# Vision tower on one core: a step's matrix work reordered around the score blocks, slot results a step later, the second key and query halves as paired 64-row products

## The reference, cut to what matters

```python
h = patches(x) @ W.T                                   # (64, 196, 768) -> (64, 196, 192)
q, k, v = silu(h @ Wq), silu(h @ Wk), silu(h @ Wv)      # 12 heads of 16
out = ((q @ k.T) * decay) @ v                           # decay: causal, exp(slope * distance)
out = layernorm((out * sigmoid(h @ Wg1 @ Wg2)) @ Wo, ln_w, ln_b)
h = layernorm(h + out)
xn = rms_norm(h) * norm_weight
logits = (l2_normalize(slots) * scale) @ l2_normalize(xn).T     # (64 slots, 196 tokens)
y = softmax(logits, over tokens) @ xn                   # 64 slot inputs for each image
y = gelu(y @ fc1[s] + fc1_bias[s]) @ fc2[s] + fc2_bias[s]       # weights of their own for each slot
h = layernorm(h + softmax(logits, over slots).T @ y)
```

## Time and profile before

| | |
|---|---|
| median of 3 runs | 1220.68 us (1220.43 to 1223.71) |
| the profiled execution, its own time | 1220.71 us |
| its span from first to last instruction | 1219.0 us |
| busy, share of the span | PE 91%, DVE 65%, ACT 62%, POOL 49% |
| phase 1 | from the start to about 938 us |
| mean granted TensorE clock | 0.958 of 2.4 GHz |

### The profile page before, as it was taken

How to read it: one execution, slowest core, us unless ns; L and a number is a source line. 1 busy time by engine, 2 the same in 40 slices (tenths; PEclk the granted TensorE clock), 3 DMA queues, 4 the chain that set the end, 5 groups by cost and what they waited for, 6 DMA issues and landing times.

```text
span 1219.0 us, 35974 instructions
## 1 busy us (share of the span) xinstructions
PE 1105.5 (91%) x13418; PEld 889.2 (73%) x13418; DVE 787.8 (65%) x2082; ACT 750.0 (62%) x1745; POOL 595.9 (49%) x942
## 2 busy tenths in 40 slices
PE   4899999999999999999999999999998999997563
PEld 3787888888888888888888888788886556564332
DVE  5577766677777777676777777777774222222996
ACT  5567677777777776777777777776763111110676
POOL 3366655565555666555655555665533000000664
PEclk9999999999999999999999999999999999998555
DMA  4411121111111111211111111112063999995786
GB/s 151 197 51 55 58 84 59 62 53 53 53 53 53 53 53 55 80 66 61 55 53 53 53 53 53 53 53 77 32 263 129 368 424 423 424 423 181 235 264 183
DMA packets 50718, 158.41 MB, mean 130 GB/s; under 512 B 5386, under 2 KB 31392, under 8 KB 38372
## 3 DMA queue, kind: packets, MB, share of 16 engines
q1 hardware_dynamic: 33080, 145.09, 32.2%
q10 hardware_dynamic: 17600, 12.78, 3.4%
HBM read 132.23 MB, written 25.62 MB: 129 GB/s over the span
## 4 chain that ended last, share of the span: by engine, by line
PE 71%; DVE 22%; issue 2%; ACT 1%; DVEq 1%; SPq 1%; DMA 1%; POOL 0%; ACTq 0%; POOLq 0%
DVE p_sb L828 9%; PE ps L974 8%; PE ps L976 7%; PE ps L975 7%; PE ps L1271 6%; PE ps L1052 5%; PE ps L1089 4%; PE ps L1290 4%; PE ps L1134 4%; DVE gn L803 3%; PE ps L1031 3%; PE ps L1032 3%; PE ps L1019 2%; PE ps L1157 2%; DVE res L943 2%
## 5 line engine op out<-in xcount | busy, mean ns | idle before, releaser
L427 POOL TENSOR_TENSOR xl<-x_sb,xh 128x392 fp32r<-128x392 f32 x192 | 189.8, 1026 | 84.1 <-DVE gn L803 74.9
L828 DVE TENSOR_TENSOR p_sb<-ps,dec 98x1568 f32<-98x1568 f32 x96 | 171.6, 1788 | 14.8 <-PE ps L1052 14.8
L678 ACT ACTIVATE hg<-ps 128x768 f32<-128x768 f32 x32 | 25.9, 810 | 146.0 <-PE ps L1295 146.0
L768 DVE BATCH_NORM_STATS2 st<-ps 98x6 f32<-98x192 f32 x128 | 40.0, 354 | 77.5 <-PE ps L1019 77.5
L935 DVE COPY y2st<-ps 128x192 f32<-128x192 f32 x32 | 11.4, 358 | 120.5 <-PE ps L1271 120.5
L695 ACT ACTIVATE o_sb<-res,nb,rstd 98x192 f32<-98x192 f32 x128 | 59.5, 535 | 44.8 <-DVE nb L958 44.1
L1089 PE MATMUL ps<-p_sb,vpad 98*32 98x98 f32 x3072 | 84.9, 250 | 1.6 <-DVE p_sb L828 1.6
L1319 PE MATMUL ps<-y2b,cbuf 64*98 64x192 f32 x256 | 49.3, 537 | 38.1 <-POOL y2b L532 38.1
L1089 PEld LDWEIGHTS ps<-p_sb,vpad 98*32 98x32 f32 x3072 | 64.1, 109 | 26.7 <-issue 26.2
L519 POOL CAST pickb<-pick 128x128 fp32r (+1 forms) x32 | 9.4, 293 | 148.8 <-PE ps L1295 148.8
L974 PE MATMUL ps<-xl,wh 128*128 128x392 f32 x192 | 70.1, 365 | 13.1 <-POOL xl L427 13.1
(11 more groups left out here) (203 smaller groups left out, 3484.8 us busy)
## 6 DMA issues: line engine op xcount, KB each, us to landing
x_sb<-in_xT SPq DMA_DIRECT2D x32, 1176.0 KB, 5.2
w1v<-in_fc SPq DMA_DIRECT2D x32, 1152.0 KB, 10.2
w2v<-in_fc SPq DMA_DIRECT2D x32, 1152.0 KB, 12.7
h_dram<-h SPq DMA_DIRECT2D x32, 294.0 KB
h2r<-h_dram SPq DMA_DIRECT2D x32, 294.0 KB
out<-o_sb ACTq DMA_DIRECT2D x32, 294.0 KB
comb_dram<-cst SPq DMA_DIRECT2D x32, 98.0 KB, 1.7
cbuf<-comb_dram SPq DMA_DIRECT2D x32, 98.0 KB, 3.8
```

What stands on the lines that cost most here:

```text
L427: pool.tensor_tensor(xl[:, k], x_sb[:, k], xh[:, k].bitcast(F32), ALU.subtract)\
L828: dve.tensor_tensor(dst, src, rate.unsqueeze(2).to_broadcast([T, 4, 2, TOK]), ALU.mult)\
```

## The change

Five edits:

1. **The last 64 features are summed.** ACT copies rows 64 to 127 of bank 1 to `kA[0:64]`, DVE adds rows 0 to 63 to that copy, twice, into rows 0 to 63 and rows 64 to 127 of `hT[:, 1]` (`summed_h`); ACT rounds that as before; POOL instead of DVE takes the rest. The weights stay as they are for keys and queries; those of the values have zeros in their second 64 rows.
2. **Keys and queries in one block.** `projected(i)` does the 12 products over the first 128 features into four banks, then the turned second half of `h` (64-row products in two row groups), then the second halves: 12 products of 64 rows each, alternately on rows 0 to 63 (first 128 outputs) and rows 64 to 127 (the other outputs), each pair into two banks.
3. **Another order of PE's work** between the score blocks; `slot_inputs_turned` and `combine_turned` of a pair come one step later (`i-3`, flag `e`), between the score blocks; `logits_turned` is two transposes instead of four products.
4. **Tokens at the next step:** `tokens` (`gn`) of a pair are made at the start of step `i` for pair `i-2`, not late in step `i-1`; with them go the squares on ACT (into a tile of their own, `ysq`), the inverse norms on POOL and the transfer of the combine weights.
5. **The start and the end:** in `step(0)` the halved output weights and the normalised slots are made after the attention work, not before it; the last two steps have a PE order of their own.

```diff
-V_AT = (2, 7)
+K_AT, Q_AT, V_AT = (2, 0), (3, 1), (4, 5)
# SP
             def step(i, d, e):
                 if d:
                     store_h2(i - 2)
                 load_x(i + 2)
-                if d:
-                    store_comb(i - 2)
+                if e:
+                    store_comb(i - 3)
# POOL, step
+                if a:
+                    low_h(i, 0)
+                if c:
+                    first_norm(i - 1, 0)
+                if d:
+                    scaled_tokens(i - 2)
+                if a:
+                    low_h(i, 1)
+                if c:
+                    first_norm(i - 1, 1)
                 if d:
                     inverse_norms(i - 2)
...
+                if more:
+                    split_x(i + 1, range(KP // 2))
                 if a:
                     pool.wait_ge(q_sb, 2 * i + 1)
...
+                if c:
+                    token_scales(i - 1)
                 if more:
-                    if c:
-                        pool.wait_ge(gn_rdy, 4 * i)
-                    split_x(i + 1, range(KP))
-                if c:
-                    token_scales(i - 1)
+                    split_x(i + 1, range(KP // 2, KP))
# ACT, step, after ogh and second_norm
+                    turned_h(i)
+                    if d:
+                        squares(i - 2)
                 if d:
                     act.wait_ge(tokT_mm, i - 1)
                     act.activation(tokT[:, :, :], ps[0:G, 6:8, 0:PT], ACT.Copy).then_inc(tokT_sb, 1)
...
+                    act.wait_ge(hT_mm, 2 * i + 2)
+                    act.activation(kA[0:64, :], ps[64:128, 1, 0:PT], ACT.Copy).then_inc(hlo_sb, 1)
                     use_table(ACT.Silu)
-                    turned_h(i, 1)
+                    act.wait_ge(hx_rdy, 2 * i + 2)
+                    act.activation(hTh[:, 1], hT[:, 1], ACT.Copy).then_inc(hTh_rdy, 1)
+                    if more:
+                        round_x(i + 1, 0)
+                    act.wait_ge(k_mm, 2 * i + 1)
+                    act.activation(kA[:, :], ps[:, K_AT[0], 0:PT], ACT.Silu).then_inc(k_sb, 1)
... (qA x2)
+                    turned_v(i, 0)
                     act.wait_ge(q_mm, 2 * i + 2)
-                    for row in (0, ZT):
-                        act.activation(zs[row:row + RANK, :], ps[DB:DB + RANK, 1, 0:PT], ACT.Copy).then_inc(zh_rdy, 1)
+                    act.activation(zs[0:GZ, :], ps[DB:DB + GZ, Q_AT[1], 0:PT], ACT.Copy).then_inc(zh_rdy, 1)
+                    turned_v(i, 1)
... (kB x2, qB x4)
+                    if e:
+                        combine_kept(i - 3, 0, f)
+                    if more:
+                        round_x(i + 1, 1)
... (gate)
                 if d:
                     use_table(ACT.Exp)
-                    exponentials(i - 2)
-                    dispatch(i - 2, d_before)
+                    slot_exponentials(i - 2)
+                    if a and e:
+                        slot_inputs_kept(i - 3, 1, 0)
+                    dispatch(i - 2)
+                    if a:
+                        token_exponentials(i - 2)
# DVE
+            def summed_h(i):
+                dve.wait_ge(hlo_sb, i + 1)
+                for x in range(2):
+                    dve.tensor_tensor(hT[64 * x:64 * x + 64, 1], ps[0:64, 1, 0:PT], kA[0:64, :],
+                                      ALU.add)                        .then_inc(hx_rdy, 1)
... (DVE step: mean_shifts(i-2), ogl x2, tokens(i-2), first_norm(i-1,0), residual(i-1,0), summed_h(i),
...  residual_statistics(i-1,0), first_norm(i-1,1), token_norms(i-2), residual(i-1,1), statistics,
...  cosine_scales(i-2), zl, hb, decay(i,0), kts, cosines(i-2), decay(i,1), slot_maxima(i-2), state,
...  decay(i,2), slot_sums(i-2), gated(i,0), shifted_logits(i-2), gated(i,1), token_sums(i-2))
# PE
+            def projected(i):
+                pe.wait_ge(hTl_rdy[0], i + 1)
+                for banks, hi, lo, groups, done in (KEYS, QUERIES):
+                    for bank, m in zip(banks, groups):
+                        if bank == Q_AT[1]:
+                            pe.wait_ge(hx_rdy, 2 * i + 2)
+                        product(ps[0:m.stop - m.start, bank, 0:PT], hi[:, 0, m], lo[:, 0, m], hTh[:, 0], hTl[:, 0],
+                                True, False)
+                h_turned(i, 1)
+                pe.wait_ge(hTl_rdy[1], i + 1)
+                for banks, hi, lo, groups, done in (KEYS, QUERIES):
+                    for w, h in ((hi, hTl), (lo, hTh), (hi, hTh)):
+                        for g, (bank, m) in enumerate(zip(banks, groups)):
+                            rows = slice(64 * g, 64 * g + 64)
+                            last = w is hi and h is hTh
+                            mm = pe.matmul(ps[0:m.stop - m.start, bank, 0:PT], w[rows, 1, m], h[rows, 1],
+                                           start=False, stop=last)
...
             def logits_turned(j):
                 pe.wait_ge(Lt_rdy, j + 1)
                 for k in range(2):
-                    for a in range(2):
-                        mm = pe.matmul(ps[64 * a:64 * a + 64, 0, k * T:(k + 1) * T],
-                                       Lt[0:T, 2 * a + k, :], ident[0:T, 0:T], start=True, stop=True)
+                    mm = pe.transpose(ps[:, 0, k * T:(k + 1) * T], Lt[0:T, 2 * k:2 * k + 2, :], ident[0:T, 0:T])
...
+            def full_step(i, c, d, e):
+                embed(i, 0, c, e)
+                if c:
+                    project_out(i - 1, 0)
+                if d:
+                    token_features(i - 2)
+                embed(i, 1, c, e)
+                if c:
+                    project_out(i - 1, 1)
...
+                projected(i)
+                if c:
+                    pe.wait_ge(t1_rdy, 4 * i)
+                rows_of_v(i, 0)
+                rows_of_v(i, 1)
+                h_turned(i, 0)
+                scores(i, 0, c)
+                pe.wait_ge(hb_sb, i + 1)
+                if d:
+                    logits(i - 2)
+                keys_turned(i)
+                if e:
+                    combine_turned(i - 3, 0)
+                scores(i, 1, c)
+                if e:
+                    pe.wait_ge(cb_sb, i - 2)
+                gate(i)
+                if d:
+                    pe.wait_ge(Lt_rdy, i - 1)
+                values(i, 0)
+                states(i)
+                if d:
+                    pe.wait_ge(g_sb, 2 * i + 1)
+                    logits_turned(i - 2)
+                scores(i, 2, c)
+                carried_ready(i)
+                values(i, 1)
+                if e:
+                    pe.wait_ge(g_sb, 2 * i + 2)
+                    slot_inputs_turned(i - 3, 1, 0)
+                carried(i, 0)
+                if d:
+                    dispatch_turned(i - 2)
+                values(i, 2)
+                if d:
+                    pe.wait_ge(g_sb, 2 * i + 2)
+                    if e:
+                        pe.wait_ge(yT_sb, 2 * i - 4)
+                    slot_inputs(i - 2)
+                carried(i, 1)
```

More of the change, by code:

```diff
@@ L1170, in h_turned @@
[L1170 removed]
                     mm.then_inc(ht_mm, 1)
[L1173 to L1175 removed]
+                else:
+                    pe.wait_ge(hx_rdy, 2 * i + 2)
+                    for mt in range(2):
+                        for a in range(2):
+                            rows, at, n = slice(64 * a, 64 * a + 64), mt * D + 128, (2 * a + mt) * T
+                            mm = pe.matmul(ps[0:T, 6 + a, at:at + 64], hT[rows, 1, n:n + T],
+                                           ident[rows, rows], start=True, stop=True)
```

418 lines of the change are left out of this document (198 added, 220 removed).

## The result

The changed kernel takes 1178.97 us in the median of its runs (1174.83 to 1180.63), the kernel before 1220.85 beside it; the ratio is 0.9647 [0.9618, 0.9676]. It is 42 us faster, where 61.7 were forecast: inside the range of 1141 to 1184, 20 us above the number.

What follows compares the result with a forecast made beforehand. PE bounds the kernel. Its slots of 25.4 us plus waits of 0.05, 0.25, 0.1 and 0.2 make 26.0 a step; 1220.7 - 60.6 - 1.2 (start) + 0.4 (end) gives 1159, range 1141 to 1184, chance about 0.8.

Steps and rivals of the forecast that it cites:

- The pairs: Key and query second halves: six pairs of 64-row products overlap, 1.08 us in place of 2.15, saving 1.07 a step.
- Rival 3: 64-row pairs do not overlap: 27.1 a step, 1193; half case, weight loads in series, 1165; chance 0.08 for both.
- The turned half: Turned second half of `h` on PE: 0.64 us becomes 0.42 with a boundary, saving 0.22 a step.
- The order and what comes with it: PE's step: holes of 0.91 and 0.15 go, `logits_turned` as two transposes saves 0.25, waits of 0.05, 0.25, 0.1, 0.2 come.
- Chain A: Second half of `h` through ACT, DVE and POOL: ready 3.75 us after `project_out(i-1,1)` starts; PE waits about 0.05.
- B: Into the first scores: PE waits 0.25 for the value blocks' silu, then 0.1 before the logits for `hb`.
- C: Chain between score blocks over DVE: 2.84 us a link; PE waits 0.2 before the third scores, elsewhere none.
- Rival 4: Slower than before: `summed_h` starts late on DVE behind POOL's `rstd`; 28.5 us a step, 1236; chance 0.05.
- the edges of the new block: Switches between 128-row and 64-row PE work in the key and query block: 0.05 us a step, range 0.05 to 0.15.
- Step 1: First step after step 0, without slot part: gains perhaps 0.5 us less than the 1.97 of a repeated step.
- The end: Last two steps: tokens and norms in step 32 +1, `tokT` earlier in step 33 -0.7, moved blocks; +0.4 us in all.
- rival 2: More waits than counted in each step, from a late `rstd` or table load: 0.8 more, 26.8 us, 1184; chance 0.20.

Runs made afterwards that it cites:

- e4: Changed kernel with both second-half products of a pair on rows 0 to 63, so they cannot overlap: 1210.42 us, step 27.23.
- e15: e5 with the wait of e10 added (POOL's first differences wait for DVE's cosine scale): 1207.51 us, step 27.18.
- e9: Changed kernel with POOL's first three differences waiting for DVE's second residual in step 1 alone: 1171.58 us.
- e3: Changed kernel with POOL's first three differences waiting for DVE's second residual in all steps: 1389.43 us.
- e5: Changed kernel's new order with the old second halves, unsummed and 128 rows high, turned half and value weights included: 1423.28 us.
- e16: Kernel before the change without POOL's wait on `gn_rdy` ahead of its six differences: 1393.63 us.
- e10: Changed kernel with the wait of e9 in step 1 and, in later steps, POOL's first differences waiting for DVE's cosine scale: 1173.61 us.
- e13: Changed kernel with the edits of e2 and e9 together: 1166.72 us.
- e14: e13 with 24 idle PE products of 128 columns ahead of the turned slots in step 0: 1167.58 us.
- e2: Changed kernel with the second norm of pair 30 put back ahead of ACT's slot copies, `tokT` and squares in step 32: 1169.59 us.

## Why the prediction came out as it did

**Steps 2 to 31: right, 5.0 us short.** Forecast 26.0, measured 26.16. The terms one by one:
- The pairs: 1.07 forecast; six at 0.18 in the trace, and 1.07 when undone (e4). Rival 3 is out, its half case with loads in series too.
- The turned half: 0.42 forecast, 0.40 measured. The order and what comes with it: -0.91, -0.15, -0.25 and the new waits of 0.6 make -0.71 forecast, -0.79 measured (e15).
- Chain A 3.75 and 3.79; B 0.25 + 0.1 and 0.23 + 0.1; C 2.84 and 2.83. Rival 4, sums of DVE that come late by microseconds, did not happen: DVE begins them 0.14 us after ACT's copy has ended. But the 0.5 us by which DVE was to be early was not there, and the sums end only 0.15 before ACT is free. "DVE idle before `summed_h`" was a wrong sign.
- Mis-sized: the edges of the new block. From the end of the last full product's slot (506.55, 0.18 after its start) to the value products (508.31) are 1.76 us, where 0.42 + 1.08 + 0.05 = 1.55 were forecast. The 0.21 is what e15 finds too: it puts the summed form at 1.02, where 1.07 + 0.22 - 0.05 = 1.24 were forecast. The order's 0.08 more makes up for part of it.
- A reading to put right: the 0.08 us of the prediction for 98 loaded columns is the slot of a `pick` product. The weight load itself takes 0.165 to 0.167 in the trace of before. The pairs' 0.18 does not hang on it.

**Step 1: the failed step, 6.6 us.** I treated it as one more step with 0.5 less gain, 24.0 us. Two things were left out.

First, what the wait on `gn_rdy` had kept apart. I counted POOL's three differences as moved and asked only whether they end in time for PE, not which operations of DVE they would now lie beside. e9, e3, e5, e15 and e16 show that the meeting is what costs: 3.6 us in step 1, and in kernels where it falls into each step 135 (e16, by its fastest run) to 205 us (e5 against e15, by the ratios). In the changed kernel the wait went and three differences moved ahead in one edit; e9 and e10 show that a wait at the new place mends it, and no run tells the two apart. The Trainium skill (SBUF — State Buffer, SBUF: two separate sides) has this rule: a VectorE operation with two SBUF inputs and a GpSimd operation that reads SBUF need the same port pair, and whichever starts first holds it for its whole instruction while the other stands. The runs agree on who is held. How long differs from case to case: the cosine scale of e3 stood through four POOL instructions in a row (3.31 us), not through one, and step 1's first residual operation through three. But in e16 DVE and POOL took turns, one instruction each (POOL's six took 6.56 in place of 5.92), and in the repeated step the held residual got in between `invn` and the first difference. No run here shows what decides between the two. Applied to the diff, the rule would have asked of the dropped wait what it kept apart.

Second, the clock, for which the forecast has no term at all. Step 1 also has no slot part, so the first link of chain C lacks the logits and the combine block with which I filled it. In e13, with the residual mended, PE still waits there (PE's timeline):

```profile
63.60 0.92 PE L1145 MATMUL ps<-qA,kA 32*98 32x196 f32 x16 [1.34 <-DVE p_sb L891]
...
70.54 0.89 PE L1178 MATMUL ps<-p_sb,vpad 98*32 98x98 f32 x32 [0.80 <-DVE p_sb L891]
```

These waits by themselves are no more than those of step 1 before: 0.24 + 1.34 + 0.80 = 2.4 us in e14, where the kernel before has 1.09 + 0.91 + 0.79 = 2.8. What step 1 keeps over 24.0 is half clock, as the busy time by stretch of e14 and then of e9 shows (the clock is the third number from the end):

```profile
65.10:68.50 3.40, 3.40 (x74) 2.76 (x72) 1.84 (x2) 1.04 (x3) 3.40 (x4) 0.50 0.00 0
```

```profile
48.40:69.98 21.58, 18.83 (x296) 15.37 (x295) 15.32 (x34) 11.00 (x23) 13.56 (x19) 1.00 0.40 158
```

In e14, 3.4 us at 0.50, begun 1.2 us after that wait, cost half of their length, 1.7 by my estimate: the step is 1.6 over 24.0. In e9 the clock is 0.50 up to 48.40, for the first 5.4 us of the step, which makes 2.7 of 3.0, and stays at 1.00 through the same wait of 1.34. e13 has both kinds (3.2 and 3.4 us at 0.50), 3.3 of 3.1. In the changed kernel 4.8 us (from 46.74) and 6.9 us (68.5 to 75.4) are at 0.50 and 0.51, the second behind the stands of 2.07 and 1.16: some 5.8 of the 6.6 us by the same estimate. So most of what the late `hb` costs is paid in clock.

**Before step 1: 3.0 us off in the profiled execution.** Forecast -1.2, measured +1.8 there and -1.0 by the median of five kernels with the same start. The size was right; one execution is a poor measure of this stretch.

**The end: the other failed step, 6.5 us.** I had +0.4 with bounds -1 and +2, and had seen `second_norm` in step 33 only, where moving `tokT` ahead of it helps. In step 32 the same move puts `second_norm(30)` behind the slot copies, `tokT` and the squares of ACT, of which the first wait 5.18 us for PE, and pair 31's first norm has to wait for it, since it writes the tile `t` that the second norm reads. e2 shows it: one condition, 7.1 us. With it steps 32 and 33 up to the first expert product take 29.0 us (859.88 to 888.86), 0.3 less than before, so my +0.4 for the rest was within a microsecond.

Had both edges come as forecast, the sum would have been near 1164 by the profiled stretches; e13 measures 1166.7. That the time lies in the range at all is in part luck: its upper bound was rival 2, more waits in every step, which gives nearly the measured time for the wrong reason, since the waits were not in every step.

What stays open: why the granted clock falls where it does in the first 45 us and behind one stand of 1.34 us and not behind another, and so what the position of the slots' norm is worth to a microsecond.

## What to carry to other kernels

When a change removes a wait because no data needs it any more, ask what it kept apart: list the operations of DVE with two SBUF inputs that the freed POOL work will now meet, and place the POOL work where it meets none. Walk each special step (first, second, last two) by itself with its own queue order; here the repeated step was forecast within 1%, and mending two stretches that pass once gave 12 us more on top of 42. Give the clock a term: in these kernels, with PE 96 to 99% busy otherwise, a stand of 1.4 to 3.4 us in each step made the step some 8 us longer, since the clock fell behind it.

## What the runs showed of the hardware

- DVE operations with two SBUF inputs were held by POOL's: 3.83, 4.06 (two residuals), 3.31 (a scale of 98x4) and 4.46 us (four `gn`), against 0.75, 0.75, 0.14 and 1.40. One was held through three or four POOL instructions in a row (step 1, e5, e3), others took turns with them (e16). Operations of DVE with one input from PSUM beside the same POOL instructions kept their time (`hb` 0.96 at 511.30, while POOL's differences ran from 509.45 to 512.54).
- A POOL operation on 98x4 elements (`invn`, 1.13 us) holds it too: the residual beside it took 1.50.
- After stands of PE of 2.1 to 3.4 us the sixteen score products took 1.48 to 1.64 us in place of 0.92, the 1.2 GHz level. Granted clock over 100 to 800 us by the stand in each step: 1.4 us 0.77 (e5), 2.3 us 0.78 (e3), 3.35 us 0.79 (e16); 0.91 us 1.00 (before), 0.23 us 1.00 (changed). A single stand of 1.34 us in step 1 was followed by 0.50 in e13 and e14, and not in e9.
- Two products of 64 rows and 392 columns, one on each half of the rows, take 0.18 us together, as one of 128 rows; undone, 0.36.
